# Quaternion sums in three GpSimd instructions of 256 elements, the key sum in one VectorE instruction, and a guard made by ScalarE

## Chip, cores and metric

The kernel runs on one core of a Trainium2 chip. The metric is device time in microseconds (us); the time before is the median of 3 runs. TensorE, VectorE, ScalarE, GpSimd and SyncE each work through their own queue in order and wait for each other on semaphores.

## What is computed

Three layers on x of 2 batches x 4096 tokens x 256 channels, float32: half a feed-forward, a memory layer, half a feed-forward. The change lies in the memory layer.

```python
# feed-forward (before and after): xr, xk mix a token with the one before it
x = x + 0.5 * (sigmoid(xr @ W_r) * (square(relu(xk @ W_k)) @ W_v))      # of layernorm(x)
# memory layer, of h = layernorm(x), quaternions of (r, i, j, k), 64 to a token
keys   = (h @ Wk.T + bk).reshape(B, L, 64, 4)
keys   = keys / maximum(norm(keys, axis=-1), 1e-12)
values = (h @ Wv.T + bv).reshape(B, L, 64, 4)
memory = cumsum(quat_mul(values, keys), axis=1)                          # over the tokens
ret    = quat_mul(memory, quat_conj(keys)) / sqrt(position)
x      = x + h + (layernorm(ret) * ln_g + ln_b) @ Wo.T + bo
```

## The kernel before

The residual x stays in SBUF for the whole run. Three stages follow each other: feed-forward 0, memory, feed-forward 1. Feed-forward stages go in 16 steps of 512 tokens (`ffn`), the memory stage (`mem`, one on each engine) in 32 steps. Step s = 2j + b is the pair j of 128-token tiles, tiles i = 0 and 1, of batch b. The first two and the last two rounds (of two steps each) are written out, the 24 steps between run in a loop; `has` says which neighbours exist. Every engine's order within a step is written out by hand in its `body`, so that order is what an engine can wait behind.

The weights are laid out by component: a tile's 256 channels are four runs of 64, one for r, i, j and k (Q = 64). VectorE makes all 16 products of two quaternions in one instruction of 1024 elements (`all_products`, L567): `bind` from values and khat, `retrieve` from the memory's running sum and khat. A product then has to be summed: `bind_sum` into `bound`, `ret_sum` into `ret`, each as two halves (`ha`, `hq`) and a total. `additions` issues a list of additions and subtractions (L222 is its line for all of them). A bind sum is 4 + 2 instructions of 64, 128 or 192 elements, a ret sum 5 + 1 of 64 to 256.

In step s:
- VectorE (L604): `key_unit(s+1)`, statistics of the residual of s+3, `bind(s+1, 0)`, `retrieve(s, 0)`, statistics of ret (s-1), `bind(s+1, 1)`, `ln_moments`, **ret_halves(s, 0)**, `ln_variance` (n_var), **ret_total(s, 0)**, `ln_inverse` (n_rstd, waits for ScalarE's root of n_var), **key_max(s+2)**, `retrieve(s, 1)`, `ln_scales` (n_shift), `key_inverse(s+2)`.
- GpSimd (L994): `ret_sum(s-1, 1)`, `bind_sum(s+1, 0)`, **key_sum(s+2)** (squares of the key, two instructions: 512 to 256 to 128 elements for both tiles), `bind_sum(s+1, 1)`.
- ScalarE (L844): `ret_normalize(s-2)`, evictions of the transposes, `store_x`, `add_normalized`, `key_square(s+2)` (ksq), `std` (n_std), **key_norm(s+2)** (root of the sum), `normalize(s+3)` (m_xn, waits for n_shift).
- TensorE (L1202): `sum_upto(s, 0)` and `sum_after(s-1, 1)` (running sum of bound), `transposes(s+2)` of m_xn, `ret_transposes(s-2)`, `project_keys(s+2)`, `sum_after(s, 0)` (waits for retrieve), `sum_upto(s, 1)`, `project_values(s+2)`, `output(s-2)`.

At the end of the memory stage GpSimd issues `inverse_std` for feed-forward 1, and then `ret_sum(NP - 1, 1, 1)` (L1014 to L1016); ScalarE's `normalize` (xn, L704) and TensorE's transposes (L1062) follow on it. wkv is loaded by one DMA (L299), bias3 is copied from PSUM by one ScalarE instruction (L889).

Of the kernel before, what the change touches and what calls it, by code (L numbers as in the profile page):

```python
# [56 lines left out]
def macaron(nc, x, w_kv, w_o, w_r, w_k, w_v, columns, out):  # L57
# [12 lines left out]
    with ExitStack() as ctx:  # L70
# [66 lines left out]
        ksum = sb("ksum", [P, 2, 2 * Q])  # L137
# [82 lines left out]
        def additions(engine, operations, done):  # L220
            for o, a, b, op in operations:
                last = engine.tensor_tensor(o, a, b, op)  # L222
            last.then_inc(done, 1)
# [18 lines left out]

        def bind_total(engine, j, b, i):
# [3 lines left out]
            ha, hq = bhalf[:, i, 0, :, :], bhalf[:, i, 1, :, :]  # L247
            out4 = bound[:, b, i, :].rearrange("p (c n) -> p c n", n=Q)
            additions(engine,
                   [(out4[:, 0:1, :], ha[:, 0:1, :], hq[:, 0:1, :], ALU.subtract),  # L250
                    (out4[:, 1:4, :], ha[:, 1:4, :], hq[:, 1:4, :], ALU.add)],
                   bound_done[i])
# [5 lines left out]
        def ret_halves(engine, j, b, i):  # L258


# [3 lines left out]
            p, ha, hq = rprod[:, i, :, :], rhalf[:, i, 0, :, :], rhalf[:, i, 1, :, :]  # L264
            additions(engine,
                   [(ha[:, 0:1, :], p[:, 0:1, :], p[:, 5:6, :], ALU.add),
                    (ha[:, 1:4, :], p[:, 4:13:4, :], p[:, 1:4, :], ALU.subtract),
                    (hq[:, 0:1, :], p[:, 10:11, :], p[:, 15:16, :], ALU.add),
                    (hq[:, 1:4:2, :], p[:, 14:8:-5, :], p[:, 11:5:-5, :], ALU.subtract),
                    (hq[:, 2:3, :], p[:, 7:8, :], p[:, 13:14, :], ALU.subtract)],  # L270
                   rhalf_done[i])

        def ret_total(engine, j, b, i):
# [15 lines left out]
        def _(sp):  # L289
# [33 lines left out]
        def _(dve):  # L323
# [156 lines left out]
            def mem():  # L480
# [123 lines left out]
                def body(j, has, start_last):  # L604
                    for b in range(2):
# [670 lines left out]
```

## Time and profile before

| | |
|---|---|
| time, median of 3 runs | 720.98 us (720.77 to 721.0) |
| profiled execution: its own time, its span | 720.35 us, 718.6 us |
| busy over the span: PE, DVE, ACT, POOL | 652.3, 613.9, 414.1, 569.9 us |
| granted TensorE clock, mean | 0.983 of full speed |
| memory stage | about 176 to 545 us |
| first matmul that reads wkv | 181.60 us |
| VectorE's third block of statistics (x loaded behind wkv) | 20.53 us, no idle time before it |
| ScalarE's copy to bias3 | 21.91 to 22.71 us; its next instruction at 23.08 |
| DMA, mean | 26 GB/s, nearly all of it before 40 us and after 540 us |

In the profile PE is TensorE, PEld its weight load, DVE VectorE, ACT ScalarE, POOL GpSimd, SP SyncE. L222 is line 222 of the kernel. A name like `kact` or `xn` in a row is the storage: `bound` lies in kact, the bind products in xn, the ret products in gating_buffers. Durations overlap by some hundredths from one instruction to the next, so the cost of one is read from start to start. Memory matmuls of float32 show as two records each.

### The profile page before, as it was taken

Reading aid. Unit: us, or ns where it says so; the run is one execution under the profiler, and the core shown is the slowest. Engines: PE = TensorE matmul, PEld = TensorE weight load, DVE = VectorE, ACT = ScalarE, POOL = GpSimd, SP = SyncE. Lnnn points to the kernel's source line nnn. Section 1 sums busy time; section 2 is a strip of 40 time slices with the busy share of each in tenths; the row PEclk is TensorE's granted clock in tenths of the full one; section 3 lists DMA queues with packets and bytes.
Section 4 is the critical chain, followed back from the end, with each engine's and each line's share of the span. In section 5 each row is a group of like instructions: output and inputs, shape, how many; then the busy total and the mean of one; then the engine's idle time right before and its main releaser. Section 6 shows DMA issues by size and latency. Waiting matters only on the chain. (4 is left out here: it accounts for less than half of the span.)

```text
span 718.6 us, 13029 instructions
## 1 busy us (share of the span) xinstructions
PE 652.3 (91%) x3536; PEld 541.8 (75%) x3536; DVE 613.9 (85%) x1378; ACT 414.1 (58%) x743; POOL 569.9 (79%) x879
## 2 busy tenths in 40 slices
PE   2999999999778988988988989989967999999997
PEld 2899998898556766766766766767756898999986
DVE  5878877765699999999999999999995877788764
ACT  4667777665435455454454454554526776677762
POOL 3788889875578888888888888888883689888873
PEclk9999999999989999999999999999988999999999
DMA  7720000000000000000000000000000011111112
GB/s 256 240 63 0 0 0 0 0 1 1 0 2 0 1 0 0 0 0 0 0 0 0 0 0 0 0 0 0 2 1 0 25 36 58 58 58 58 37 51 89
DMA packets 18442, 18.67 MB, mean 26 GB/s; under 512 B 752, under 2 KB 18160, under 8 KB 18416
## 3 DMA queue, kind: packets, MB, share of 16 engines
q1 hardware_dynamic: 18416, 18.36, 7.8%
q8 instruction: 12, 0.20, 0.1%
q14 instruction: 14, 0.11, 0.1%
HBM read 9.97 MB, written 8.39 MB: 26 GB/s over the span
## 5 line engine op out<-in xcount | busy, mean ns | idle before, releaser
L222 POOL TENSOR_TENSOR bhalf<-xn 128x128 f32<-128x128 f32 x256 | 118.1, 492 | 30.0 <-DVE xn L567 30.0
L1135 PE MATMUL bank<-wkv,m_xnT 128*128 128x256 f32 x512 | 134.9, 394 | 5.5 <-DVE khat L561 4.1
L1079 PE MATMUL bank<-wffn,kact 128*128 128x256 f32 x512 | 117.0, 381 | 1.6 <-DVE kact L402 1.6
L1135 PEld LDWEIGHTS bank<-wkv,m_xnT 128*128 128x128 f32 x512 | 92.2, 196 | 25.3 <-issue 4.5
L1079 PEld LDWEIGHTS bank<-wffn,kact 128*128 128x128 f32 x512 | 94.7, 190 | 13.9 <-issue 1.1
L284 POOL TENSOR_TENSOR xk_lo<-xk,xk_hi 128x1024 fp32r<-128x1024 f32 x30 | 71.0, 2368 | 31.9 <-ACT xk_hi L712 31.9
L946 POOL TENSOR_TENSOR xr_lo<-xr,xr_hi 128x1024 fp32r<-128x1024 f32 x32 | 76.2, 2381 | 18.1 <-ACT xr_hi L718 16.4
L953 POOL TENSOR_TENSOR res<-res,gating_buffers 128x1024 f32 (+1 forms) x31 | 75.4, 2433 | 9.1 <-DVE gating_buffers L409 8.6
L567 DVE TENSOR_TENSOR xn<-bank,khat 128x1024 f32<-128x1024 f32 x64 | 77.8, 1216 | 1.4
L567 DVE TENSOR_TENSOR gating_buffers<-bank,khat 128x1024 f32<-128x1024 f32 x64 | 77.6, 1212 | 0.0
L1046 PE MATMUL bank<-wffn_hi,xr_hi 128*128 128x256 f32 x256 | 71.4, 279 | 0.3 <-ACT res L819 0.3
L1046 PE MATMUL bank<-wffn_hi,xr_lo 128*128 128x256 f32 x256 | 71.2, 278 | 0.0
L1046 PE MATMUL bank<-wffn_lo,xr_hi 128*128 128x256 f32 x256 | 71.2, 278 | 0.0
L222 POOL TENSOR_TENSOR rhalf<-gating_buffers 128x64 f32<-128x64 f32 (+2 forms) x160 | 58.8, 402 | 13.7 <-DVE gating_buffers L567 13.7
L704 ACT ACTIVATE xn<-res,shift,rstd 128x256 f32 (+1 forms) x128 | 66.6, 594 | 4.4 <-POOL shift L941 4.3
L386 DVE TENSOR_TENSOR diff<-bank,xnT 128x1024 f32<-128x1024 f32 x32 | 39.2, 1224 | 34.9 <-ACT xnT L695 34.9
L1183 PE MATMUL bank<-wo,normedT 128*128 128x256 f32 x256 | 67.5, 387 | 1.5 <-ACT normedT L825 1.5
L409 DVE TENSOR_TENSOR gating_buffers<-bank,gating_buffers 128x1024 f32<-128x1024 f32 x31 | 38.0, 1225 | 35.3 <-ACT gating_buffers L730 25.3
L768 ACT ACTIVATE n_std<-n_var 128x4 f32<-128x4 f32 (+1 forms) x36 | 7.4, 205 | 105.3 <-DVE n_var L524 105.3
L776 ACT ACTIVATE m_xn<-res,n_shift,n_rstd 128x256 f32 (+1 forms) x64 | 34.9, 592 | 50.5 <-DVE n_shift L538 50.5
L222 POOL TENSOR_TENSOR kact<-bhalf 128x64 f32<-128x64 f32 (+1 forms) x128 | 56.0, 459 | 6.0 <-PE bank L1162 1.9
L718 ACT CAST xr_hi<-xr 128x1024 fp32r<-128x1024 f32 x32 | 33.5, 1046 | 43.2 <-DVE xr L394 43.2
(108 smaller groups left out, 1663.0 us busy)
## 6 DMA issues: line engine op xcount, KB each, us to landing
res<-x SPq DMA_DIRECT2D x16, 512.0 KB, 4.4
out<-res SPq DMA_DIRECT2D x15, 512.0 KB, 2.9
wkv<-w_kv SPq DMA_DIRECT2D x1, 512.0 KB, 7.3
out<-res SPq DMA_DIRECT2D x2, 256.0 KB, 2.2
wffn<-w_k SPq DMA_DIRECT2D x1, 256.0 KB, 3.9
wffn<-w_r SPq DMA_DIRECT2D x1, 256.0 KB, 4.1
wffn<-w_v SPq DMA_DIRECT2D x1, 256.0 KB, 4.6
wo<-w_o SPq DMA_DIRECT2D x1, 256.0 KB, 6.6
```

What stands on the lines that cost most here:

```text
L222: last = engine.tensor_tensor(o, a, b, op)
L284: ops.tensor_tensor(xk_lo[:, :, :], xk[:, :, :], xk_hi[:, :, :].bitcast(F32), ALU.subtract).then_inc(e["xklo_done"], 1)
L386: nc.vector.tensor_tensor(diff[:, :, :], xT_ps, xnT[:, b, :, 0:CW], ALU.subtract).then_inc(e["diff_done"], 1)
L409: nc.vector.tensor_tensor(gated, v_tok, gate, ALU.mult).then_inc(e["gated_done"], 1)
L567: nc.vector.tensor_tensor(dst[:, i, :, :].rearrange("p (a b) n -> p a b n", a=4), of.rearrange("p (a n) -> p a n", n=Q).unsqueeze(2).to_br ...
L704: last = nc.scalar.activation(xn[:, b, i, :], t[:, i, :], ACT.Identity, bias=shift[:, b, i:i + 1], scale=rstd[:, b, i:i + 1])
L946: nc.gpsimd.tensor_tensor(xr_lo[:, :, :], xr[:, :, :], xr_hi[:, :, :].bitcast(F32), ALU.subtract).then_inc(e["xrlo_done"], 1)
L953: nc.gpsimd.tensor_tensor(t, t, gated, ALU.add).then_inc(e["res_done"], 1)
L1046: last = nc.tensor.matmul(out_ap, w(f), v(f), start=k == 0, stop=k == n - 1)
L1079: last = nc.tensor.matmul(dst[:, i, :], x[:, f, i * P:(i + 1) * P], wffn[:, w, f, :], start=f == 0, stop=f == FC - 1)
L1135: nc.tensor.matmul(dst[:, i, :], m_xnT[:, f, i * P:(i + 1) * P], wkv[:, f, col:col + D], start=f == 0, stop=False)
L1183: nc.tensor.matmul(o_bank[:, i, :], normedT[:, f, i * P:(i + 1) * P], wo[:, f, :], start=f == 0, stop=False)
```

## The change

- The two halves of a sum become one instruction of 256 elements each, whatever the signs. `picked` makes one operand of four of the 16 products, in a 2 x 2 x 64 pattern; the first half is a subtraction, the second an addition, and the total an addition of 256: three instructions a sum.
- For that the third and fourth component of the keys change places in wkv and bias3: wkv is loaded by four DMAs, bias3 copied by four ScalarE instructions.
- All four sums of a step are on GpSimd: `ret_sum(j, b, 0)` moves there from VectorE, between the two bind sums.
- `key_sum` moves from GpSimd to VectorE, as one `tensor_reduce` over the four components, between `ln_moments` and `ln_variance`.
- `key_max` is gone; ScalarE makes the guard: relu(sum - 1e-24), then the root of that + 1e-24. It waits on its own first result.
- VectorE's `key_inverse` waits for `knorm_done`.

```diff
+BIND_PLUS, BIND_MINUS, BIND_REST = (5, 3, 12, 10), (0, 6, 9, 15), ((11, 8, 7, 4), (14, 13, 2, 1))
+RET_PLUS, RET_MINUS, RET_REST = (13, 1, 14, 2), (0, 6, 9, 15), ((7, 12, 3, 8), (10, 11, 4, 5))
+def picked(products, slots):
+    a, b, c, d = slots
+    assert a + d == b + c
+    n = products.shape[-1]
+    first = products[:, a, :]
+    return bass.AP(tensor=first.tensor, offset=first.offset,
+                   ap=[list(first.ap[0]), [(c - a) * n, 2], [(b - a) * n, 2], [1, n]])
...
-            p, ha, hq = bprod[:, i, :, :], bhalf[:, i, 0, :, :], bhalf[:, i, 1, :, :]
-            additions(engine,
-                   [(ha[:, 0:3:2, :], p[:, 0:3:2, :], p[:, 5:8:2, :], ALU.subtract),
-                    (ha[:, 1:4:2, :], p[:, 1:4:2, :], p[:, 4:7:2, :], ALU.add),
-                    (hq[:, 0:3:2, :], p[:, 10:14:3, :], p[:, 15:7:-7, :], ALU.add),
-                    (hq[:, 1:4:2, :], p[:, 11:13:1, :], p[:, 14:8:-5, :], ALU.subtract)],
-                   bhalf_done[i])
+            p = bprod[:, i, :, :]
+            engine.tensor_tensor(quarters(bhalf[:, i, 0, :]), picked(p, BIND_PLUS), picked(p, BIND_MINUS), ALU.subtract)
+            engine.tensor_tensor(quarters(bhalf[:, i, 1, :]), picked(p, BIND_REST[0]), picked(p, BIND_REST[1]),
+                                 ALU.add).then_inc(bhalf_done[i], 1)
...
+            engine.tensor_tensor(bound[:, b, i, :], bhalf[:, i, 0, :], bhalf[:, i, 1, :], ALU.add).then_inc(bound_done[i], 1)
...
-            sp.dma_start(wkv[:, :, :], w_kv.rearrange("(f p) n -> p f n", p=P)).then_inc(wkv_in, 16)
+            w_kv_rows = w_kv.rearrange("(f p) n -> p f n", p=P)
+            sp.dma_start(wkv[:, :, 0:2 * Q], w_kv_rows[:, :, 0:2 * Q]).then_inc(wkv_in, 16)
+            sp.dma_start(wkv[:, :, 2 * Q:3 * Q], w_kv_rows[:, :, 3 * Q:4 * Q]).then_inc(wkv_in, 16)
+            sp.dma_start(wkv[:, :, 3 * Q:4 * Q], w_kv_rows[:, :, 2 * Q:3 * Q]).then_inc(wkv_in, 16)
+            sp.dma_start(wkv[:, :, D:], w_kv_rows[:, :, D:]).then_inc(wkv_in, 16)
...
-                    nc.vector.tensor_scalar(knorm[:, :, :], knorm[:, :, :], NORM_EPS, None, ALU.max).then_inc(m["kmax_done"], 1)
+                def key_sum(j, b):
+                    s = 2 * j + b
+                    dve.wait_ge(m["ksq_done"], s + 1)
+                    need(dve, m["above_done"], s)
+                    nc.vector.tensor_reduce(ksum[:, :, :], ksq[:, :, :].rearrange("p t (c n) -> p t n c", n=Q),
+                                            mybir.AxisListType.X, ALU.add).then_inc(m["ksum_done"], 1)
...
                         ln_moments(s + 3, *where)
-                        ret_halves(nc.vector, j, b, 0)
+                        if has(b, 2):
+                            key_sum(j + 1, b)
                         ln_variance(s + 3, *where)
-                        ret_total(nc.vector, j, b, 0)
                         ln_inverse(s + 3, *where)
-                        if has(b, 2):
-                            key_max(j + 1, b)
                         retrieve(j, b, 1)
...
                     act.wait_ge(m["ksum_done"], s + 1)
+                    nc.scalar.activation(above[:, :, :], ksum[:, :, :], ACT.Relu, bias=minus_least[:, :]).then_inc(m["above_done"], 1)
+                    act.wait_ge(m["above_done"], s + 1)
                     need(act, m["kinv_done"], s)
-                    nc.scalar.activation(knorm[:, :, :], ksum[:, :, 0:Q], ACT.Sqrt).then_inc(m["knorm_done"], 1)
+                    nc.scalar.activation(knorm[:, :, :], above[:, :, :], ACT.Sqrt, bias=least[:, :]).then_inc(m["knorm_done"], 1)
...
                             bind_sum(nc.gpsimd, *at(j, b, 1), 0)
-                        if has(b, 2):
-                            key_sum(j + 1, b)
+                        ret_sum(nc.gpsimd, j, b, 0)
                         if has(b, 1):
                             bind_sum(nc.gpsimd, *at(j, b, 1), 1)
```

## Rows read from the trace of the kernel before

**Rows 1.** The page, part 1: busy us, share of the span, instructions.
```profile
PE 652.3 (91%) x3536; PEld 541.8 (75%) x3536; DVE 613.9 (85%) x1378; ACT 414.1 (58%) x743; POOL 569.9 (79%) x879
```
**Rows 2.** Windows view, memory stage: window, us, busy of PE, PEld, DVE, ACT, POOL.
```profile
250.00:490.00 240.00, 218.20 (x1101) 167.80 (x1100) 237.03 (x551) 122.62 (x264) 203.67 (x441) 1.00 0.00 0
```
**Rows 3.** Source view of L524: durations in ns, first and last start.
```profile
L524 DVEq FUSED_REGOPS  x24: 65/73/82, 246.9 to 498.0; - x24
```
**Rows 4.** Timeline of one step, VectorE: start us, duration us, instruction [idle before].
```profile
312.31 1.88 DVE L222 TENSOR_TENSOR rhalf<-gating_buffers 128x64 f32<-128x64 f32 x5
...
314.12 0.43 DVE L524 TENSOR_TENSOR n_var<-n_mv,eps 128x4 f32<-128x4 f32 x1
...
314.81 0.18 DVE L530 RECIPROCAL n_rstd<-n_std 128x4 f32<-128x4 f32 x1
315.01 0.27 DVE L548 TENSOR_SCALAR knorm<-knorm 128x128 f32<-128x128 f32 x1
315.20 1.21 DVE L567 TENSOR_TENSOR gating_buffers<-bank,khat 128x1024 f32<-128x1024 f32 x1
...
317.54 0.69 DVE L561 TENSOR_TENSOR khat<-bank,kinv 128x512 f32<-128x512 f32 x1
...
318.15 0.74 DVE L490 BATCH_NORM_STATS2 n_st<-res 128x6 f32 x2
```
**Rows 5.** Timeline of TensorE, one step without a wait and the next.
```profile
230.14 0.59 PE L1155 MATMUL bank<-kact,upto 128*128 128x256 f32 x2
...
231.01 0.60 PE L1129 MATMUL bank<-ident,m_xn 128*128 128x128 f32 x4
...
239.96 0.59 PE L1155 MATMUL bank<-kact,upto 128*128 128x256 f32 x2
...
241.38 0.66 PE L1129 MATMUL bank<-ident,m_xn 128*128 128x128 f32 x4 [0.39 <-ACT m_xn L776]
```
**Rows 6.** Timeline at the start of the memory stage: n_var and what GpSimd does.
```profile
180.75 2.35 POOL L953 TENSOR_TENSOR res<-res,gating_buffers 128x1024 f32<-128x1024 f32 x1 [6.52 <-DVE gating_buffers L409]
...
181.64 1.47 DVE L524 TENSOR_TENSOR n_var<-n_mv,eps 128x2 f32<-128x2 f32 x1
...
184.80 0.16 DVE L524 TENSOR_TENSOR n_var<-n_mv,eps 128x2 f32<-128x2 f32 x1
...
185.23 0.17 DVE L530 RECIPROCAL n_rstd<-n_std 128x2 f32<-128x2 f32 x1 [0.27 <-ACT n_std L768]
```
**Rows 7.** Groups by form on GpSimd, 250 to 500 us: busy us, mean ns | idle.
```profile
L222 POOL TENSOR_TENSOR bhalf<-xn 128x128 f32<-128x128 f32 x183 | 85.0, 495 | 20.0 <-DVE xn L567 20.0
...
L222 POOL TENSOR_TENSOR ret<-rhalf 128x256 f32<-128x256 f32 x23 | 16.7, 728 | 2.8 <-POOL rhalf L222 1.9
...
L222 POOL TENSOR_TENSOR rhalf<-gating_buffers 128x128 f32<-128x128 f32 x23 | 10.5, 458 | 0.0
```
**Rows 8.** Timeline of ScalarE: the key's square, and the next normalisation.
```profile
234.54 0.60 ACT L799 ACTIVATE ksq<-bank 128x512 f32<-128x512 f32 x1 [0.21 <-PE bank L1137]
...
316.69 1.09 ACT L776 ACTIVATE m_xn<-res,n_shift,n_rstd 128x256 f32 x2 [1.71 <-DVE n_shift L538]
```
**Rows 9.** Timeline of VectorE in step 0: the halves of ret.
```profile
202.13 2.57 DVE L222 TENSOR_TENSOR rhalf<-gating_buffers 128x64 f32<-128x64 f32 x5
```
**Rows 10.** Timeline of the hand-over to feed-forward 1.
```profile
535.58 0.20 POOL L936 TENSOR_TENSOR minus_mean<-mv,minus_one 128x4 f32<-128x4 f32 x1
...
536.31 1.19 DVE L567 TENSOR_TENSOR gating_buffers<-bank,khat 128x1024 f32<-128x1024 f32 x1
...
537.11 0.20 POOL L941 TENSOR_TENSOR shift<-minus_mean,rstd 128x4 f32<-128x4 f32 x1
...
539.51 2.06 ACT L704 ACTIVATE xn<-res,shift,rstd 128x256 f32<-128x256 f32 x4
...
541.63 1.97 PE L1062 MATMUL bank<-ident,xn 128*128 128x128 f32 x8 [2.17 <-ACT xn L704]
```
**Rows 11.** Timeline of ScalarE: the table load before the memory stage.
```profile
176.97 1.28 ACT L679 ACT_TABLE_LOAD   x1
```

More of the change, by code:

```diff
@@ L102, in macaron @@
         eps_tile = sb("eps_tile", [P, CT])
+        least = sb("least", [P, 1])
+        minus_least = sb("minus_least", [P, 1])
         spare = sb("spare", [P, 1])
@@ L136, in macaron @@
         ksq = sb("ksq", [P, 2, D])
-        ksum = sb("ksum", [P, 2, 2 * Q])
+        ksum = sb("ksum", [P, 2, Q])
+        above = sb("above", [P, 2, Q])
         knorm = sb("knorm", [P, 2, Q])
@@ L143, in macaron @@
         rprod = gating_buffers[:, :, :].rearrange("p i (c n) -> p i c n", n=Q)
-        bhalf = sb("bhalf", [P, 2, 2, 4, Q])
-        rhalf = sb("rhalf", [P, 2, 2, 4, Q])
+        bhalf = sb("bhalf", [P, 2, 2, D])
+        rhalf = sb("rhalf", [P, 2, 2, D])
         bound = kact[:, :, :].rearrange("p b (t n) -> p b t n", n=D)
@@ L217, in macaron, with quarters @@
         block = ctx.enter_context(nc.Block())
[L220 to L223, printed above, removed]
+        def quarters(ap):
+            return ap.rearrange("p (y x n) -> p y x n", y=2, x=2)
         def bind_sum(engine, j, b, i):
@@ L246, in bind_total @@
             need(engine, after_done[i], s - 1)
[L247 to L252, printed above, removed]
+            engine.tensor_tensor(bound[:, b, i, :], bhalf[:, i, 0, :], bhalf[:, i, 1, :], ALU.add).then_inc(bound_done[i], 1)
         def ret_sum(engine, j, b, i):
@@ L263, in ret_halves @@
             need(engine, ret_done[i], s)
[L264 to L271, printed above, removed]
+            p = rprod[:, i, :, :]
+            engine.tensor_tensor(quarters(rhalf[:, i, 0, :]), picked(p, RET_PLUS), picked(p, RET_MINUS), ALU.subtract)
+            engine.tensor_tensor(quarters(rhalf[:, i, 1, :]), picked(p, RET_REST[0]), picked(p, RET_REST[1]),
+                                 ALU.add).then_inc(rhalf_done[i], 1)
         def ret_total(engine, j, b, i):
@@ L276, in ret_total @@
             need(engine, m["normed_done"], s - 1)
-            additions(engine, [(ret[:, b, i, :], rhalf[:, i, 0, :, :].rearrange("p c n -> p (c n)"),
-                                rhalf[:, i, 1, :, :].rearrange("p c n -> p (c n)"), ALU.add)], ret_done[i])
+            engine.tensor_tensor(ret[:, b, i, :], rhalf[:, i, 0, :], rhalf[:, i, 1, :], ALU.add).then_inc(ret_done[i], 1)
         def key_low(engine, ops, e, j, b):
@@ L594, in first_bind @@
                 def first_bind():
-                    key_max(0, 0)
+                    key_sum(0, 0)
                     key_inverse(0, 0)
@@ L599, in first_bind @@
                     bind(0, 0, 1)
-                    key_max(0, 1)
+                    key_sum(0, 1)
                     key_inverse(0, 1)
@@ L888, in _ @@
             act.wait_ge(bias_rows_ready, 1)
-            nc.scalar.copy(bias3[:, :], v_flat[:, 0:3 * D]).then_inc(bias_rows_ready, 1)
+            nc.scalar.copy(bias3[:, 0:2 * Q], v_flat[:, 0:2 * Q])
+            nc.scalar.copy(bias3[:, 2 * Q:3 * Q], v_flat[:, 3 * Q:4 * Q])
+            nc.scalar.copy(bias3[:, 3 * Q:4 * Q], v_flat[:, 2 * Q:3 * Q])
+            nc.scalar.copy(bias3[:, D:], v_flat[:, D:3 * D]).then_inc(bias_rows_ready, 1)
             ffn_steps()
@@ L913, in prepare @@
                 nc.gpsimd.memset(eps_tile[:, :], LN_EPS)
+                nc.gpsimd.memset(least[:, :], NORM_EPS ** 2)
+                nc.gpsimd.memset(minus_least[:, :], -NORM_EPS ** 2)
                 nc.gpsimd.iota(pos[:, :], pattern=[[P, NT]], base=1, channel_multiplier=1).then_inc(consts_pool, 1)
@@ L976, in mem @@
             def mem():
-                def key_sum(j, b):
-                    s = 2 * j + b
-                    pool.wait_ge(m["ksq_done"], s + 1)
-                    need(pool, m["knorm_done"], s)
-                    nc.gpsimd.tensor_tensor(ksum[:, :, :], ksq[:, :, 0:2 * Q], ksq[:, :, 2 * Q:4 * Q], ALU.add).then_inc(m["khalf_done"], 1)
-                    pool.wait_ge(m["khalf_done"], s + 1)
-                    nc.gpsimd.tensor_tensor(ksum[:, :, 0:Q], ksum[:, :, 0:Q], ksum[:, :, Q:2 * Q], ALU.add).then_inc(m["ksum_done"], 1)
                 pool.wait_ge(ffn_sems[0]["xr_done"], FC * NS)
                 nc.gpsimd.memset(xnT[:, :, :, 0:1], 0.0).then_inc(shift_zeroed, 1)
-                key_sum(0, 0)
                 bind_sum(nc.gpsimd, 0, 0, 0)
-                key_sum(0, 1)
                 bind_sum(nc.gpsimd, 0, 0, 1)
@@ L1187, in output @@
                     last.then_inc(m["O_done"], 1)
-                pe.wait_ge(wkv_in, 16)
+                pe.wait_ge(wkv_in, 16 * 4)
                 pe.wait_ge(mem_ready, 1)
```

6 lines of the change are left out of this document (2 added, 4 removed).

## Prediction

> **What bounds the kernel now.** I read the shares of the engines first, then the memory stage alone, then one of its steps row by row on each engine. Over the span TensorE is busiest [rows 1], but that is a mean over three stages. In 240 us of the memory stage VectorE is busy 237.03 us, 98.8%, TensorE 218.20 and GpSimd 203.67 [rows 2]. The stage has 32 steps (a pair of tiles of one batch each). The step's own register instruction on VectorE comes 24 times between 246.9 and 498.0, so one step takes 251.1/23 = 10.92 us [rows 3]. In a step VectorE's instructions follow each other without an idle entry [rows 4], while TensorE's rows show it waiting 0.39 us for m_xn in a step of this kind [rows 5]: VectorE sets the step. TensorE is close behind, and one step shows by how much: from the sum_upto at 230.14 to the next one at 239.96 it never waited, and that took 9.82 us [rows 5]. So TensorE's floor is 9.82 us a step, and what VectorE gives up beyond 1.10 us a step is worth nothing. The first and last stages (feed-forward) are TensorE's own and the change doesn't enter them but at two points, costed below.
>
> **VectorE, per step.** Removed: the five instructions of rhalf, 312.31 to 314.12, 1.81 us; and the maximum on knorm, 315.01 to 315.20, 0.19 us [rows 4]. The sum ret goes too, but it stood between n_var and n_rstd, where VectorE has to wait for ScalarE's square root: n_var to n_rstd took 314.12 to 314.81, 0.69 us, with it [rows 4]. Without anything between them and with GpSimd idle the same pair took 184.80 to 185.23, 0.43 us [rows 6]. Added: one tensor_reduce over 512 elements, which no row shows. The nearest row is khat, also 512 float32 elements in one instruction: 317.54 to 318.15, 0.61 us to the next start [rows 4]; I take 0.61. The low end is that same row less nothing, since no row of VectorE does an element faster than this one; the high end is half its rate, 1.21 us, which is what the 1024 elements of a product take in one instruction [rows 4]. There is a fourth term: n_var reads two SBUF tensors, and while GpSimd works such an instruction waits. At 181.64 n_var took 1.47 us and ended at 183.11, when GpSimd's instruction begun at 180.75 (2.35 us) ended [rows 6]. GpSimd's instructions become 0.73 us long [rows 7] and it will be busy nine tenths of the time, so n_var waits from 0 to 0.73 us, on the mean about 0.33.
> So VectorE's step is 10.92 - 1.81 - 0.19 - 0.69 + 0.43 + 0.61 + 0.33 = 9.60 us, between 9.27 (no wait) and 10.60 (both terms at their high ends). At 9.60 it is below TensorE's 9.82.
> The Trainium skill has a rule that speaks against the change: SBUF — State Buffer, section "SBUF: two separate sides", calls the port pair of the two engines an exclusive lock, held by a GpSimd instruction to its end, against a VectorE instruction with two SBUF inputs. By that rule the trace agrees (the 1.47 us), and it would make the term at most one GpSimd instruction, as above; the same rule frees VectorE's step of five more such waits, since rhalf is gone. The skill's VectorE: DVE Perf Modes, "The perf-mode tier table", gives tensor_reduce only the 1x mode; no run here shows it.
>
> **GpSimd, per step.** Its time for one instruction is linear in the elements: 128 take 0.458 us and 256 take 0.728 [rows 7]. The forms with one and two runs of 64 in them lie on the same line as the contiguous one of 256, so I charge strides with nothing. A sum becomes two halves and a total: 0.69 + 0.73, then 0.07 us for the wait on its own semaphore, then 0.73: 2.22 us. Four sums a step (ret 1, bind 0, ret 0, bind 1) make 8.9 us; the key sum leaves. The high end comes from bhalf, whose 128-element form has a mean of 0.495 us beside VectorE's rhalf [rows 7]: twice that, 0.99 us for 256, makes a sum 0.99 + 0.99 + 0.07 + 0.73 = 2.78 and the step 11.1 us. That cover is VectorE's rhalf itself, which is removed, so I take 8.9, the row without it. The order holds as well. From the end of retrieve 1, ret 1 is summed by 2.3 us, and VectorE needs it only before the statistics of ret, after kinv, khat, the statistics of res and two products, 4.7 us later by the starts of those instructions. Bind 0, ret 0 and bind 1 then follow their products with at most one sum queued, and TensorE uses a bound tile one step later.
>
> **ScalarE.** The norm gets a second activation of 128 elements and a wait on it, about 0.3 us. ScalarE is busy 122.62 of 240 us [rows 2]. What is queued behind it is the normalisation m_xn, which waits for n_shift after retrieve 1, 1.2 us on; kinv on VectorE comes later still. Nothing. The new wait is VectorE's on ksq, and behind it are queued n_var, n_rstd, retrieve 1 and n_shift. In TensorE's unhindered step the transposes began at 231.01 [rows 5] and ksq at 234.54 for 0.60 us [rows 8]. From there: key sum 0.61, n_var to n_rstd 0.76, n_rstd 0.20, then retrieve 1 to m_xn 315.20 to 316.69, 1.49, and m_xn 1.09 [rows 4, 8]. Together 4.13 + 0.61 + 0.76 + 0.20 + 1.49 + 1.09 = 8.3 us, so m_xn is ready 1.5 us before TensorE asks for it at 9.82.
>
> **Costed at nothing.** Four DMAs of wkv for one: its first use is at 180 us, and the loads of x behind it on SyncE's queue are needed late (VectorE's statistics at 20.5 us didn't wait); without that cover it would be the 1 to 2 us of three more issues. Four copies of bias3 for one, about 0.3 us on ScalarE at 22 us, next to an idle stretch before the first relu; at worst 0.3. Two memsets on GpSimd before 3 us, 0.03 us each.
>
> **The edges.** Steps 0 and 1: rhalf took 2.57 us in step 0 [rows 9], and TensorE has no output matmuls there, but its clock is at half speed for part of that time; I take a gain of 2 us for both. Steps 30 and 31 have no key sum and little TensorE work, so VectorE's saving counts there: 1.5 us. But the hand-over to the last stage loses. Before, GpSimd had the first scales of that stage (shift) at 537.11, while VectorE did ret 0 of step 31; then ScalarE began xn at 539.51 and TensorE, idle, began its transposes at 541.63 [rows 10]. Now GpSimd's queue has ret_sum(31, 0) ahead of those scales: retrieve 0 ends 1.2 us after 536.31, the sum takes 2.22, the scales 1.73 (535.58 to 537.31), so xn starts 5.2 us after 536.31 and not 3.2 [rows 10]. This chain ends last; it costs 2.0 us in full.
>
> **The sum.** The bound becomes TensorE at 9.82 us, and I add 0.05 for small waits: 9.87. Steps 2 to 29 are 28: 28 x (10.92 - 9.87) = 29.4 us. With 2 + 1.5 - 2.0 the gain is 30.9 us. The profiled execution took 720.35 us, 0.63 below the median of 720.98: 720.35 - 30.9 = 689.4, against the median 690.1. I say 690.
>
> **The rivals.**
> 1. VectorE stays the bound. This needs 0.22 us more than my 9.60, for instance n_var waiting for a whole GpSimd instruction (10.00) or a reduce at half rate (10.20); with both, 10.60. For it: neither price is in the trace. Against it: the reduce must be slower per element than all VectorE rows but the reciprocals. With 10.1 to 10.6 the steps save 23 to 9 us, and with the edges 696 to 710; typically 698. Chance 0.25.
> 2. GpSimd becomes the bound, and the kernel slower. The place is its queue of four sums a step; it decides from 10.92/4 = 2.73 us a sum, 0.51 above my price, so if a half of 2 x 2 x 64 elements with uneven steps costs 0.98 us and not 0.73. At the high end, 11.1, it is 28 x 0.2 = 6 us slower, and 2 for the hand-over: 728. Against it: three forms with other numbers of runs are on one line. Between 2.46 and 2.73 it still gains less than forecast, 693 to 720. Chance 0.08 altogether, half of it slower.
> 3. Table reloads on ScalarE: if Relu weren't in the table that Sqrt uses, each step would have two loads of 1.28 us [rows 11], the key norm would come some 1.2 us after VectorE wants it, and a step would take 10.8: about 718. Against it: in the memory stage Square, Copy, Identity and Sqrt alternate after a single load. Chance 0.02. The Trainium skill, ScalarE: Activation LUTs, "Table sets: the hidden batching unit", says relu is in every set, which would rule this out.
>
> **How the numbers follow.** My forecast (TensorE the bound, 684 to 693) has 0.65. Its low end is 9.82 flat with 3 us more from the early steps, where VectorE's waits go too. To hold 8 in 10 the range must take in most of rival 1: 684 to 704. A measurement of this kernel tells about 0.2% (1.4 us) from no change. Faster: 0.65 + 0.25 + 0.04 + 0.01, about 0.95; within 0.2%: 0.01; slower: 0.04.
>
> **What would show it.** In a step of the new trace: TensorE without waits on ScalarE and 9.8 us from one sum_upto(0) to the next; VectorE with an idle entry before the key sum, released by ksq; the key sum at 0.7 us busy; n_var between 0.15 and 0.88 us; GpSimd's halves at 0.73 us each; at the hand-over shift ending 5.1 us after retrieve 0 of step 31 begins. I'm wrong if VectorE shows no idle time in the middle of the stage (rival 1), if GpSimd shows none (rival 2), or if the table load appears more often than before.

## The result: 704.2 us, and VectorE is still the bound

The changed kernel took 704.22 us (median of 4 runs, 703.37 to 705.0) against 720.88 us for the kernel before in the same series: a ratio of 0.976, with a 95% interval of 0.975 to 0.978. It is 16.7 us faster where 30.9 us were forecast. That is the first rival of the prediction, VectorE stays the bound, and not the forecast. The profiled execution took 705.0 us, with a span of 703.3 us.

The page of the changed kernel, part 1 (busy us, share of the span, instructions), answers to [rows 1]:
```profile
PE 649.1 (92%) x3536; PEld 544.0 (77%) x3536; DVE 586.8 (83%) x1186; ACT 429.6 (61%) x778; POOL 544.9 (77%) x625
```
The windows view of its memory stage (window, its us, busy PE, PEld, DVE, ACT, POOL, then granted clock, DMA share, GB/s) answers to [rows 2], and the source view of VectorE's register instruction (durations in ns, first and last start) to [rows 3]:
```profile
240.00:480.00 240.00, 228.53 (x1164) 179.39 (x1164) 231.10 (x441) 141.91 (x304) 196.76 (x279) 1.00 0.00 0
L532 DVEq FUSED_REGOPS  x24: 65/70/89, 244.0 to 481.6; - x24
```
The step is 237.6/23 = 10.33 us, where it was 10.92 [rows 3] and 9.87 was forecast. GpSimd is busy 82% and is no bound; TensorE is busy 95.2% but VectorE 96.3%. The waits view of the same stretch shows that TensorE waits for ScalarE, in each of the 23 steps for `normed` and in 20 of them for `m_xn`; both are made from VectorE's n_shift:
```profile
PE bank L1175 <- ACT normed L824: 7.5, 23, 0.3
PE bank L1133 <- ACT m_xn L785: 3.5, 20, 0.3
```
So VectorE ends the step. Read what it does. One step of it in the changed kernel, from the timeline (start us, duration us, instruction, [idle before]), and below it GpSimd at the same time; these answer to [rows 4]:
```profile
305.54 0.37 DVE L523 BATCH_NORM_AGGREGATE n_mv<-n_st 128x2 f32<-128x6 f32 x4
305.83 1.02 DVE L558 TENSOR_REDUCE ksum<-ksq 128x128 f32<-128x512 f32 x1
306.76 0.49 DVE L532 TENSOR_TENSOR n_var<-n_mv,eps 128x4 f32<-128x4 f32 x1
307.53 0.18 DVE L538 RECIPROCAL n_rstd<-n_std 128x4 f32<-128x4 f32 x1 [0.27 <-ACT n_std L777]
307.62 1.21 DVE L578 TENSOR_TENSOR gating_buffers<-bank,khat 128x1024 f32<-128x1024 f32 x1
308.75 0.72 DVE L545 TENSOR_SCALAR n_gain<-n_rstd 128x2 f32<-128x2 f32 x1
309.38 0.15 DVE L546 SCALAR_TENSOR_TENSOR n_shift<-n_mv,n_rstd 128x4 f32<-128x4 f32 x1
309.46 0.94 DVE L565 RECIPROCAL kinv<-knorm 128x128 f32<-128x128 f32 x1
```
```profile
307.19 0.74 POOL L254 TENSOR_TENSOR bhalf<-xn 128x256 f32<-128x256 f32 x1
...
308.72 0.73 POOL L262 TENSOR_TENSOR kact<-bhalf 128x256 f32<-128x256 f32 x1
309.40 0.73 POOL L274 TENSOR_TENSOR rhalf<-gating_buffers 128x256 f32<-128x256 f32 x1
```
VectorE's only idle entry is 0.27 us, at n_rstd. Read the starts down the column: the key sum takes 0.93 us to the next start (0.61 in the sum), n_var to n_rstd 0.77 (0.76 in the sum; 0.73 on the mean of the loop's steps), and n_gain, an instruction on 2 elements, takes 0.63 where it took 0.06 before (316.34 to 316.40). It starts at 308.75, 0.03 us behind the start of GpSimd's total (308.72), and ends within 0.02 us of that total's end (309.45). So it is in each of the 22 steps between 245 and 465 us: n_gain ends 0.02 to 0.03 us after the GpSimd instruction that was running. Before, the same n_gain was at 316.34, and GpSimd had nothing to do just then, as the timelines of the kernel before show:
```profile
316.34 0.15 DVE L537 TENSOR_SCALAR n_gain<-n_rstd 128x2 f32<-128x2 f32 x1
315.27 0.87 POOL L222 TENSOR_TENSOR kact<-bhalf 128x64 f32<-128x64 f32 x2
316.49 1.84 POOL L222 TENSOR_TENSOR rhalf<-gating_buffers 128x64 f32<-128x64 f32 x5 [0.35 <-DVE gating_buffers L567]
```
Not every VectorE instruction waits. n_rstd, a reciprocal of four elements, starts at 307.53 in the middle of GpSimd's bhalf (307.19 to 307.93) and takes 0.18 us; kinv, another reciprocal, starts 0.06 us behind GpSimd's rhalf and takes 0.94, as before.

The groups by form of 240 to 480 us say that the step above is typical (busy us, mean ns | idle before; the last line but one is ScalarE's):
```profile
L558 DVE TENSOR_REDUCE ksum<-ksq 128x128 f32<-128x512 f32 x23 | 23.4, 1017 | 0.0
L545 DVE TENSOR_SCALAR n_gain<-n_rstd 128x2 f32<-128x2 f32 x23 | 16.3, 710 | 0.0
L532 DVE TENSOR_TENSOR n_var<-n_mv,eps 128x4 f32<-128x4 f32 x23 | 10.6, 460 | 0.0
L538 DVE RECIPROCAL n_rstd<-n_std 128x4 f32<-128x4 f32 x23 | 4.1, 178 | 6.2 <-ACT n_std L777 6.2
L546 DVE SCALAR_TENSOR_TENSOR n_shift<-n_mv,n_rstd 128x4 f32<-128x4 f32 x23 | 3.4, 149 | 0.0
L808 ACT ACTIVATE ksq<-bank 128x512 f32<-128x512 f32 x24 | 14.4, 598 | 0.0
L254 POOL TENSOR_TENSOR bhalf<-xn 128x256 f32<-128x256 f32 x47 | 34.8, 740 | 34.7 <-DVE xn L578 34.7
```

**Where the 15.35 us between the two profiled executions lie.** I compare the starts of the same instruction in both timelines. The first n_var of the memory stage starts at 182.87 us instead of 181.64 [rows 6]: feed-forward 0 became 1.23 us longer. From there to n_var of step 2 it gained 2.54, from step 2 to step 29 17.32, and from there to retrieve 0 of step 31 0.77. At the hand-over it lost 2.00, and from xn to the end it lost 2.08. The sum is -1.23 + 2.54 + 17.32 + 0.77 - 2.00 - 2.08 = 15.32.

The hand-over, from the timeline of the changed kernel, answers to [rows 10]:
```profile
516.91 1.19 DVE L578 TENSOR_TENSOR gating_buffers<-bank,khat 128x1024 f32<-128x1024 f32 x1
...
518.18 0.73 POOL L274 TENSOR_TENSOR rhalf<-gating_buffers 128x256 f32<-128x256 f32 x1 [1.67 <-DVE gating_buffers L578]
...
521.88 0.20 POOL L958 TENSOR_TENSOR shift<-minus_mean,rstd 128x4 f32<-128x4 f32 x1
...
522.11 2.07 ACT L713 ACTIVATE xn<-res,shift,rstd 128x256 f32<-128x256 f32 x4 [2.27 <-POOL shift L958]
...
524.24 1.97 PE L1066 MATMUL bank<-ident,xn 128*128 128x128 f32 x8 [4.58 <-ACT xn L713]
```
From retrieve 0 to xn it is 5.20 us, where it was 3.20 [rows 10]: the scales wait behind a sum that was not in this queue before. TensorE stands idle 4.58 us before these transposes, against 2.17.

### The profile page after: what moved, and what is told of

The parts are those of the page before. It is cut to its first block, busy times and chain, and to the rows that moved or that the text cites. A ratio compares the mean times of both kernels' runs of the same rounds, so it can differ in the third digit from the quotient of the medians.

```text
span 703.3 us, 12621 instructions
## 1 busy us (share of the span) xinstructions
PE 649.1 (92%) x3536; PEld 544.0 (77%) x3536; DVE 586.8 (83%) x1186; ACT 429.6 (61%) x778; POOL 544.9 (77%) x625
## 3 DMA queue, kind: packets, MB, share of 16 engines
HBM read 9.97 MB, written 8.39 MB: 26 GB/s over the span
## 4 chain that ended last, share of the span: by engine, by line
PE 24%; DVE 18%; issue 18%; POOL 4%; DVEq 1%; ACT 1%; POOLq 0%
PE bank L1050 12%; PE bank L1083 8%; DVE gating_buffers L578 4%; DVE kinv L565 3%; DVE n_st L507 2%; PE bank L1066 2%; DVE n_var L532 2%; DVE n_gain L545 2%; DVE n_mv L523 1%; DVE n_st L498 1%; PE bank L1187 1%; POOL rhalf L274 1%; DVE xn L578 1%; POOL rhalf L275 1%; POOL bhalf L254 1%
## 5 line engine op out<-in xcount | busy, mean ns | idle before, releaser
L254 POOL TENSOR_TENSOR bhalf<-xn 128x256 f32<-128x256 f32 x64 | 47.3, 740 | 52.8 <-DVE xn L578 52.8
L1187 PEld LDWEIGHTS bank<-wo,normedT 128*128 128x128 f32 x256 | 47.0, 194 | 10.5 <-ACT normedT L837 1.9
L1050 PE MATMUL bank<-xk_hi,wffn_hi 128*128 128x512 f32 x128 | 53.2, 416 | 0.0
```

The source lines that it names most:

```text
L254: engine.tensor_tensor(quarters(bhalf[:, i, 0, :]), picked(p, BIND_PLUS), picked(p, BIND_MINUS), ALU.subtract)
L1050: last = nc.tensor.matmul(out_ap, w(f), v(f), start=k == 0, stop=k == n - 1)
L1187: nc.tensor.matmul(o_bank[:, i, :], normedT[:, f, i * P:(i + 1) * P], wo[:, f, :], start=f == 0, stop=False)
```

## Experiments

All twelve compute everything that the kernel computes. "Step" is the distance of VectorE's register instructions, as in [rows 3]. The kernel before had medians of 720.4 to 720.5 us in these series, so the changed kernel's ratio of 0.976 stands for 703.5 there.

| kernel | median us | ratio (95%) | step us |
|---|---|---|---|
| the change | 704.22 | 0.976 (0.975 to 0.978) | 10.33 |
| e1_gain_act | 702.18 | 0.975 (0.973 to 0.977) | 10.26 |
| e2_bind_first | 695.29 | 0.966 (0.964 to 0.967) | 9.99 |
| e3_contiguous | 691.74 | 0.960 (0.958 to 0.961) | 9.79 |
| e7_var_first | 688.32 | 0.956 (0.954 to 0.959) | 9.80 |
| e4_least_last | 701.99 | 0.974 (0.972 to 0.975) | 10.33 |
| e5_before_shifted | 722.90 | 1.003 (1.002 to 1.004) | - |
| e6_scales_first | 701.46 | 0.973 (0.972 to 0.975) | 10.33 |
| e8_ret_vector | 723.21 | 1.003 (1.002 to 1.005) | 10.97 |
| e9_form_only | 723.06 | 1.003 (1.002 to 1.005) | 11.09 |
| e10_key_gpsimd | 698.89 | 0.970 (0.968 to 0.972) | 10.07 |
| e11_three_edits | 684.37 | 0.950 (0.948 to 0.951) | 9.80 |
| e12_four_edits | 685.32 | 0.951 (0.950 to 0.953) | 9.88 |

### n_gain waits for GpSimd: is it the instruction or its place?

**e1** takes n_gain away from VectorE and lets ScalarE make it. If n_gain has a price of its own, 0.6 us a step goes; if VectorE waits for GpSimd's instruction, the next one of its kind inherits the wait.
```diff
-                        nc.vector.tensor_scalar(n_gain[:, q, :], n_rstd[:, q, 2:4], 1.0, None, ALU.add)
...
+                    nc.scalar.activation(n_gain[:, b, :], n_rstd[:, b, 2:4], ACT.Identity, bias=one_tile[:, :]).then_inc(m["gain_done"], 1)
```


> n_gain moves from VectorE to ScalarE, nothing else. My theory: the 0.71 us of n_gain in the changed kernel is a wait for the GpSimd instruction in progress, and n_shift (two SBUF inputs) would wait for the same one. Then n_gain's wait is inherited by n_shift, which becomes about 0.7 us long; a step stays at 10.3 us and the time at 704 +- 1.5. Rival: only the form of n_gain (one SBUF input, a constant) is slow or waits. Then n_shift stays at 0.15, a step takes 9.8 to 9.9 us and the time is 690 to 693.

The group of n_shift in e1, by form:
```profile
L545 DVE SCALAR_TENSOR_TENSOR n_shift<-n_mv,n_rstd 128x4 f32<-128x4 f32 x19 | 13.3, 698 | 0.0
```
n_shift, 149 ns in the change, now takes 698. The wait changed its owner and the step lost 0.07 us, n_gain's own cost; the time, 702.2, lies 0.3 us below the expected 704 +- 1.5. So it is a wait for GpSimd and not the price of n_gain.

**e2** moves the place instead: on VectorE, bind 0 goes ahead of the statistics of res, so that everything that GpSimd gets comes at another time.
```diff
-                        ln_stats_res(s + 3, *where)
                         if has(b, 1):
                             bind(*at(j, b, 1), 0)
+                        ln_stats_res(s + 3, *where)
```


> VectorE's product bind(., 0) stands ahead of the two statistics of the residual instead of behind them, so GpSimd's run of four sums begins 0.66 us earlier against VectorE's step; the same instructions. Lock theory: GpSimd's total of bind 1 then ends about when retrieve 1 ends, n_gain falls from 0.71 to about 0.15 us, a step from 10.33 to 9.8 to 9.9 us (TensorE's 9.82 is the floor), the time to 690 to 693. Rival (n_gain's length comes from its own form, or from waiting on n_rstd): n_gain stays at 0.7, the time at 704.

The groups by form of e2:
```profile
L545 DVE TENSOR_SCALAR n_gain<-n_rstd 128x2 f32<-128x2 f32 x20 | 3.2, 158 | 0.0
L532 DVE TENSOR_TENSOR n_var<-n_mv,eps 128x4 f32<-128x4 f32 x20 | 9.9, 496 | 0.0
```
n_gain is back at 158 ns, without any change to it. The step fell by 0.34 and not by the whole 0.55: bind 0 now begins 0.72 and 0.81 us after khat in turn, where the statistics began 0.61 after it, and n_var waits a little longer. The time, 695.3, lies above the expected 690 to 693. Both runs together show the mechanism: n_var, n_gain and n_shift wait until GpSimd's running instruction ends, whichever of them lands in one, while the reciprocals n_rstd and kinv, with one input each, never wait.

The Trainium skill, SBUF — State Buffer, section "SBUF: two separate sides", states this as an exclusive lock on a port pair, held for a whole instruction, for VectorE instructions with two SBUF inputs and also for those in a two-port mode. The trace agrees for two inputs: n_shift at 698 ns. n_gain has one input and a constant and takes 710 ns; no trace here shows whether it runs in a two-port mode.

### What the key sum costs, and why

**e3** writes the squares with the four components side by side, so that the key sum reads 512 elements in a row and not with a stride of 64 elements.
```diff
-                    nc.scalar.activation(ksq[:, :, :], keys, ACT.Square)
+                    nc.scalar.activation(ksq[:, :, :].rearrange("p t (n c) -> p t c n", n=Q),
+                                         keys.rearrange("p t (c n) -> p t c n", n=Q), ACT.Square)
...
-                    nc.vector.tensor_reduce(ksum[:, :, :], ksq[:, :, :].rearrange("p t (c n) -> p t n c", n=Q),
+                    nc.vector.tensor_reduce(ksum[:, :, :], ksq[:, :, :].rearrange("p t (n c) -> p t n c", n=Q),
```


> ScalarE writes the squares with the four components of a quaternion side by side, so that the tensor_reduce reads 512 contiguous elements instead of every 64th. If the stride makes the reduce slow, it falls from 1.02 to about 0.69 us, a step to 10.0 and the time to about 695. If it is the price of reducing in groups of 4, it stays at 1.02 and the time at 704; ScalarE's square may get longer (0.60 now), up to 0.3 us without harm.

The groups by form of e3, on VectorE and on ScalarE:
```profile
L558 DVE TENSOR_REDUCE ksum<-ksq 128x128 f32<-128x512 f32 x21 | 14.0, 668 | 1.0 <-ACT ksq L808 0.7
L808 ACT ACTIVATE ksq<-bank 128x512 f32<-128x512 f32 x21 | 23.6, 1124 | 6.4 <-PE bank L1142 6.2
```
The same reduce over the same 512 elements takes 668 ns where it took 1017: the stride was the price, and without it the prediction's 0.61 would have been about right (0.59 us to the next start, on the mean). ScalarE pays for it, 598 to 1124 ns for its strided write, and that is hidden. n_gain (625 ns) and n_var (300 ns) wait less too, as they come at another time, so not all of the gain is the key sum's. It is larger than expected (691.7 against 695).

The Trainium skill, VectorE: DVE Perf Modes, "The perf-mode tier table", gives tensor_reduce the plain 1x mode. The contiguous one agrees (668 ns against 691 of khat, also 512 elements); the strided one at 1017 ns is half as long again, and no rule of that table gives that.

### The same instructions in another order

**e7** only changes places: n_var ahead of the key sum. The key sum then lies over ScalarE's square root, for which VectorE waited before.
```diff
-                        if has(b, 2):
-                            key_sum(j + 1, b)
                         ln_variance(s + 3, *where)
+                        if has(b, 2):
+                            key_sum(j + 1, b)
```


> n_var stands ahead of the key sum, so that ScalarE's square root of it is made while VectorE reduces. Theory: the idle 0.27 us ahead of n_rstd goes; n_var waits for GpSimd at another moment, from 0 to 0.7 us instead of 0.3. If that wait is unchanged the step goes from 10.33 to about 10.06 and the time to 696 to 698. Rival: the waits for GpSimd fall elsewhere and take it all back, 703 to 706.

The groups of e7, its register instruction, and the chain of work that ended last, by engine, of e7 and then of the change:
```profile
L545 DVE TENSOR_SCALAR n_gain<-n_rstd 128x2 f32<-128x2 f32 x21 | 6.4, 307 | 0.0
L532 DVE TENSOR_TENSOR n_var<-n_mv,eps 128x4 f32<-128x4 f32 x20 | 6.1, 304 | 3.2 <-DVE n_mv L523 1.7
L538 DVE RECIPROCAL n_rstd<-n_std 128x4 f32<-128x4 f32 x21 | 3.5, 166 | 0.0
L532 DVEq FUSED_REGOPS  x24: 65/70/89, 239.4 to 464.9; - x24
PE 57%; POOL 5%; ACT 3%; issue 3%; DVE 2%; POOLq 0%; DVEq 0%
```
```profile
PE 24%; DVE 18%; issue 18%; POOL 4%; DVEq 1%; ACT 1%; POOLq 0%
```
Three things became smaller at once: the 0.27 us of idle time before n_rstd is gone (0.16 come back as n_var's wait for n_mv), n_var fell by 0.16 and n_gain by 0.40 on the mean. In the timeline n_gain takes 0.60 to 0.72 us in 6 of 23 steps of the loop and 0.15 to 0.22 in the others: in this order most of them fall outside GpSimd's instructions. By the sum, 10.33 - 0.27 + 0.16 - 0.16 - 0.40 = 9.66 us is left to VectorE, and the step is 9.80, TensorE's floor. TensorE is the chain that ended last, 57% of the span; its one wait in a step, 0.24 us, is for the copy (m_xnT) of its own transposes. I had expected 696 to 698 from the idle time alone; the share of the waits for GpSimd was not in it. The loop also begins 4.6 us earlier (239.4 against 244.0), since steps 0 and 1 have the same order.

### Eight bytes

The change allocates two new tiles of 4 bytes a partition, `least` and `minus_least`, ahead of nearly all others. **e4** allocates them last; **e5** is the kernel before with 8 unused bytes at that place.
```diff
-        least = sb("least", [P, 1])
-        minus_least = sb("minus_least", [P, 1])
...
         normedT = sb("normedT", [P, FC, 2 * P])
+        least = sb("least", [P, 1])
+        minus_least = sb("minus_least", [P, 1])
```


> The two new one-column tiles (least, minus_least) are allocated behind all others, so that every tile allocated after them lies 8 bytes lower, where it lay before the change. Theory: in the feed-forward stages a step takes 9.98 us in the changed kernel and 9.91 before, because TensorE's operands lie at other addresses (receptance matmuls 284 ns instead of 278); then the step returns to 9.91, and the time falls by 1.5 to 2.5 us, to 702. Rival: the clock or the four DMAs made the difference: 704, feed-forward steps at 9.98.

```diff
         eps_tile = sb("eps_tile", [P, CT])
+        unused = sb("unused", [P, 2])
```


> The kernel before, with an unused tile of 8 bytes where the change puts its two one-column tiles. Address theory: feed-forward steps become 9.98 us instead of 9.91, and the kernel is 2.0 to 2.5 us slower than before, 723. Rival: 721, no change.

The feed-forward's matmuls, groups by form of the change, then e4, then e5:
```profile
L1050 PE MATMUL bank<-wffn_lo,xr_hi 128*128 128x256 f32 x256 | 72.6, 284 | 0.0
```
```profile
L1050 PE MATMUL bank<-wffn_lo,xr_hi 128*128 128x256 f32 x256 | 71.1, 278 | 0.0
```
```profile
L1047 PE MATMUL bank<-wffn_lo,xr_hi 128*128 128x256 f32 x256 | 71.8, 280 | 0.0
```
In feed-forward 1, from the starts of the same matmul of each step, a step takes 9.91 us before, 9.98 in the change, 9.91 in e4 and 9.97 in e5. Two times 16 steps at 0.07 make 2.2 us. The runs say the same: e5 is 2.4 us slower than the kernel before beside it, e4 2.2 us faster than the change by the medians, 1.9 by the ratios. That the shift of the addresses does it is shown; which of the shifted tiles matters, and why, is not.

### The hand-over

**e6** issues the first scales of feed-forward 1 on GpSimd ahead of ret_sum(31, 0).
```diff
+                        if not has(b, 1):
+                            scales(0, 0)
+                            scales(0, 1)
                         ret_sum(nc.gpsimd, j, b, 0)
```


> At the hand-over GpSimd makes the scales of feed-forward 1 ahead of the sum of ret 0 of step 31, everything else as in the changed kernel. My prediction charged 2.0 us for this order. Theory: xn starts 3.0 to 3.2 us after retrieve 0 of step 31 begins and not 5.2, and the time is 2.0 us lower, about 702. Rival: the later sum of ret 31 or an idle TensorE gives some of it back: 0 to 1 us.

The timeline of e6:
```profile
516.52 1.19 DVE L578 TENSOR_TENSOR gating_buffers<-bank,khat 128x1024 f32<-128x1024 f32 x1
517.61 0.20 POOL L958 TENSOR_TENSOR shift<-minus_mean,rstd 128x4 f32<-128x4 f32 x1
...
518.99 2.06 ACT L713 ACTIVATE xn<-res,shift,rstd 128x256 f32<-128x256 f32 x4
```
xn starts 2.47 us after retrieve 0 and not 5.20. The time is 2.8 us lower by the medians (2.3 by the ratios), of 2.7 on the chain.

### Which part of the change brings the gain

**e8** leaves ret 0 on VectorE, in the new form of three instructions, and has the rest of the change.
```diff
                             key_sum(j + 1, b)
+                        ret_halves(nc.vector, j, b, 0)
                         ln_variance(s + 3, *where)
+                        ret_total(nc.vector, j, b, 0)
...
-                        ret_sum(nc.gpsimd, j, b, 0)
```


> The sum of ret 0 is back on VectorE, in its new form of three instructions of 256, the key sum stays there too. Two of the three cost about 0.35 us each at least and the third lies in the wait for the square root, and all have two SBUF inputs, so each may wait for GpSimd. Theory: a step of 10.33 + 0.7 to 10.33 + 1.5 us, 11.0 to 11.8, the time 723 to 745, slower than before. Rival: GpSimd is the hidden bound and is relieved, 704 or less.

**e9** is the kernel before with the new form alone; ret 0, the key sum and the guard stay where they were.
```diff
+            engine.tensor_tensor(quarters(rhalf[:, i, 0, :]), picked(p, RET_PLUS), picked(p, RET_MINUS), ALU.subtract)
...
```


> The kernel before with the new form of the sums alone (three instructions of 256 each, with the four DMAs and copies that the order of components needs); ret 0 stays on VectorE, the key sum on GpSimd, the maximum on VectorE. VectorE's rhalf goes from five instructions (1.81 us) to two of at least 0.35 us each, each waiting for GpSimd up to 0.7 us: 0.7 to 1.9 us. Theory: a step of 9.9 to 11.0 us, by the waits seen with ret 0 on VectorE (0.65 and 0.94 us for the halves) rather 10.7, so 713 to 717. Rival: the shorter sums alone carry most of the gain, 700 to 706.

Groups by form on VectorE, of e8 (the second half of ret 0):
```profile
L275 DVE TENSOR_TENSOR rhalf<-gating_buffers 128x256 f32<-128x256 f32 x19 | 17.9, 944 | 0.0
```
and of e9, with two instructions of its GpSimd timeline:
```profile
L525 DVE TENSOR_TENSOR n_var<-n_mv,eps 128x4 f32<-128x4 f32 x18 | 12.3, 684 | 0.0
L549 DVE TENSOR_SCALAR knorm<-knorm 128x128 f32<-128x128 f32 x18 | 9.5, 530 | 0.4
...
312.26 0.92 POOL L247 TENSOR_TENSOR bhalf<-xn 128x256 f32<-128x256 f32 x1
...
319.88 0.74 POOL L247 TENSOR_TENSOR bhalf<-xn 128x256 f32<-128x256 f32 x1 [1.30 <-DVE xn L568]
```
e8 came at the low end of what was expected: without the move of ret 0 the change is 0.3% slower than the kernel before. Most of these 2.7 us are the eight bytes of e5 (2.4), which e8 has too, so without that move the rest of the change gains nothing. e9 is a miss. I had expected 713 to 717, and it is 2.5 us slower than before. In its timeline the halves take 1.47 us from start to start instead of 1.81 [rows 4], 0.34 less; but n_var to n_rstd takes 0.95 instead of 0.69 and the maximum 0.45 instead of 0.19, 0.26 more each. Together + 0.18, and the step is 0.17 longer. GpSimd's instructions are fewer but longer, so a VectorE instruction that meets one waits longer. The wait goes both ways: the bind sum that GpSimd makes beside VectorE's rhalf, n_var and ret takes 0.92, 0.90 and 0.86 us, the other one of the step 0.74, 0.74 and 0.73. The form gains nothing by itself; it pays by making room on GpSimd for the fourth sum.

**e10** brings the key sum back to GpSimd, as two instructions between bind 0 and ret 0.
```diff
-                        if has(b, 2):
-                            key_sum(j + 1, b)
                         ln_variance(s + 3, *where)
...
+                        if has(b, 2):
+                            key_sum(j + 1, b)
                         ret_sum(nc.gpsimd, j, b, 0)
```


> The changed kernel with the key sum back on GpSimd in its two instructions, between bind 0 and ret 0. GpSimd then has 8.9 + 1.35 = 10.2 us of work a step and VectorE 10.33 - 0.93 = 9.4. Theory: GpSimd becomes the bound, with a step of 10.3 to 10.8 and hardly any idle time on it: 704 to 718. Rival: VectorE remains what sets the step and gains the 0.5 us that TensorE's floor leaves, 690 to 693.

The windows view of e10, and who is waited for on VectorE:
```profile
260.00:460.00 200.00, 193.47 (x997) 154.33 (x997) 177.19 (x360) 123.36 (x259) 190.56 (x279) 1.00 0.00 0
L507 DVE BATCH_NORM_STATS2 n_st<-ret 128x6 f32<-128x256 f32 x40 | 16.9, 422 | 10.6 <-POOL ret L282 10.6
```
GpSimd is the bound here: it is busy 95% of the time and VectorE waits for its ret in every step. But with a step of 10.07, below the 10.3 to 10.8 expected, and 5.3 us less than the change (4.6 by the ratios). So in the place where the change put it, the key sum's 0.93 us on VectorE were dearer than its 1.2 us on GpSimd. With e7's order the opposite holds (688.3).

### The version that beats both

**e11** joins e4, e6 and e7; **e12** adds e2.

> The changed kernel with three of the edits that helped by themselves: least and minus_least allocated last (-2.2 us), n_var ahead of the key sum (-15.9), the scales of feed-forward 1 ahead of the last ret 0 (-2.8). They lie in different stages, so if they add up: 704.2 - 20.9 = 683.3. Rival: the hand-over's gain is smaller once the steps before it run at TensorE's pace: 685 to 686.

> The same three and bind 0 ahead of the residual's statistics as well. Theory: with n_var first a step already takes 9.80 us, TensorE's floor, so the fourth edit gives nothing: 683 to 684. Rival: it moves n_var and n_gain into GpSimd's instructions again and costs up to 0.3 us a step, 684 to 692.

The chain by engine of e11:
```profile
PE 62%; ACT 3%; DVE 3%; issue 1%; DVEq 0%
```
684.37 us (682.89 to 684.96), 5% below the kernel before and 19.9 us below the change; 683.3 was the sum of the single gains by the medians; by the ratios it is 684.6. The step is TensorE's 9.80, so what e2 frees on VectorE is worth nothing here, and e12 (685.3, step 9.88) is no better, as its rival said: n_var is back at 491 ns in it.

## Why the prediction was right or wrong

**The bound.** "It becomes TensorE at 9.82 us" was wrong for the change, by 0.5 us a step. This is the first rival, with a chance of 0.25. The floor itself was right: e3, e7 and e11 lie at 9.79 to 9.80, and no run went below.

**VectorE's step, term by term.** The forecast was 9.60, the trace shows 10.33. The measured terms are means over the loop's steps, from start to start.
- The key sum was mis-sized: 0.61, measured 0.93. I took a contiguous row for a strided read. The upper bound, 1.21, held. This is 0.32. (The sentence that no row of VectorE does an element faster than khat was wrong too, without effect: a product does 1024 elements in 1.14 us, 315.20 to 316.34.)
- n_gain and n_shift were not in the sum. This is the step of it that failed: I had the rule that a VectorE instruction with two SBUF inputs waits for GpSimd's, charged it to n_var alone, and did not go through the other small instructions and ask where GpSimd would be at their time. The rule as I had it covers n_shift but not n_gain, whose wait hides n_shift's; e1 shows that one of the two pays. Before, n_gain fell into GpSimd's gap of 0.35 us; the fourth sum fills that gap. The price is 0.56 us a step (0.63 against 0.07), and e1 and e2 show the cause.
- n_var to n_rstd was right (0.76, measured 0.73), with the 0.27 of idle time and the wait for GpSimd in it. n_rstd to retrieve 1 is 0.09 instead of 0.20.
- Sum: 9.60 + 0.32 + 0.56 - 0.03 - 0.11 = 10.34, against 10.33. The key sum and n_gain alone are 0.88 us too much.

Against the profiled execution 30.9 us were forecast and 15.35 came, 15.6 fewer. In the memory stage and at the hand-over the gain was 2.54 + 17.32 + 0.77 - 2.00 = 18.6 instead of 30.9, 12.3 fewer; the step, 10.33 instead of 9.87, makes 28 x 0.46 = 12.9 of that by itself. The other 3.3 are the feed-forward stages, below.

**GpSimd.** Right. 0.727 to 0.743 us for 256 elements in every pattern (0.728 was taken), and with a sum of some 2.2 us four fit into the step. That uneven steps cost nothing held, and the second rival did not come. That VectorE's rhalf lengthens GpSimd's instructions, as the prediction supposed when it took the row without it, is so: beside rhalf they take 0.92 us in e9, without it 0.74.

**ScalarE, DMAs, bias.** Right. The group rows of the change give 386 ns for the added activation and 402 for the root, n_std's wait for n_var (57.9 us in 240) shows that ScalarE stands idle, and there is no table load beyond those of before. The x loads begin at 7.72 us instead of 5.54 and nobody waits for them.

**The edges.** 2.5 us at the first steps (2 forecast), 0.8 at the last (1.5), and the hand-over is exact: xn 5.20 us after retrieve 0 of step 31, as forecast, and removing it gives 2.3 to 2.8 us.

**The feed-forward stages** were said to be touched at two points only. They lost 2.2 us in all their steps by an 8-byte shift of the tiles, which no step of the prediction looked at, and feed-forward 1 about another 0.9 us, between xn and its first receptance matmul (20.81 us, where it was 19.91): the windows view shows TensorE's granted clock at 0.50 (1.2 GHz) for 8 us at the hand-over, where TensorE stood idle for 2.77 us, worked for 1.5 and stood idle for 4.58, and in the second of these windows it was working:
```profile
520.00:524.00 4.00, 0.00 (x0) 0.00 (x0) 1.25 (x3) 1.89 (x4) 3.69 (x10) 0.50 0.00 0
524.00:528.00 4.00, 3.76 (x14) 3.22 (x15) 0.66 (x1) 2.87 (x6) 1.83 (x3) 0.50 0.00 0
```
In the kernel before, TensorE stood idle for 2.77 and 2.17 us and took up its work again at 541.63, also at half clock; the next window is at 0.68 on the mean:
```profile
542.00:546.00 4.00, 4.00 (x18) 3.53 (x17) 1.23 (x2) 2.87 (x6) 1.58 (x4) 0.68 0.00 0
```
Read in windows of 1 us, the half clock lasts 3.0 us into that work before, 3.7 in e6, 4.4 in e4 and 4.8 in the change, and from xn to the first receptance matmul it takes 19.91, 20.29, 20.62 and 20.81 us: half a microsecond more for each microsecond more at half clock. These are four runs in line, and none of them changes the clock alone.

**The range** ended at 704.0 and the time lies on that end: 704.22 by the median, and 0.9764 x 720.98 = 703.96 by the ratio. It reached that far only because it took in most of the first rival. The forecast itself, TensorE as the bound at 690, did not come, and that the time still lies on the end of the range is luck. The rival's typical value, 698, was too low: it counted either a whole wait at n_var or a reduce at half rate. The reduce came half of the way to that (0.93, between 0.61 and 1.21), the wait came at n_gain, and the 3.3 us of the feed-forward stages came on top.

## What to carry to other kernels

Where instructions of one engine wait for those of another, as here between VectorE and GpSimd, find out which forms do (n_var, n_gain, n_shift, not the reciprocals), list them all, and ask what the other engine runs at that moment in the new order; a gap that hides one is lost as soon as the other engine gets more work, and merging instructions makes each wait longer (e9). An instruction that is moved onto an engine is best laid over a wait that the engine has anyway: the change with its key sum ahead of n_var took 15 to 16 us more than with it behind. A strided read on VectorE needs its own row; a contiguous one of the same size is no price for it.

## What the runs showed of the hardware that I had not expected

- A tensor_reduce of 512 float32 elements takes 668 ns contiguous and 1017 ns with the four components 64 elements apart.
- ScalarE's write from PSUM with a stride of four elements takes 1124 ns, against 598 without.
- A GpSimd instruction of 256 elements takes 0.92 us beside a VectorE rhalf and 0.74 otherwise (e9), while a reciprocal of 4 elements on VectorE takes 178 ns in the middle of a GpSimd instruction (n_rstd in the change).
- Eight bytes more ahead of most tiles make the feed-forward's 256-column matmuls 280 to 284 ns long instead of 278, and a feed-forward step 9.97 to 9.98 us instead of 9.91.
- Whether VectorE's waits could be avoided by operands in PSUM was not tried.
